# Second attention of a vision tower: scores one step deep in 64-row tiles, projections and output products as jobs between the steps

## The chip, the cores and the metric

One core of one Trainium2 chip runs the whole model. The metric is the device time of one execution in microseconds (us); lower is better. TensorE (PE in the profile, PEld for its weight loads) multiplies matrices into the eight banks of PSUM, VectorE (DVE) and ScalarE (ACT) work on PSUM and SBUF, GpSimd (POOL) on SBUF alone, SyncE (SP) issues transfers. Each engine runs its own instructions in order and waits for the others at semaphores.

## The reference

An image batch of 8 gives 8 x 64 tokens of width 192. A vision-transformer block, a mixture of four attention experts, a mixture of eight feed-forward experts, a second attention and class-wise experts follow, with layer norms between. The change touches the four attention experts:

```
def _L0_attn_ref(x, wq, wk, wv, wo, w_gate, w_up):
    ...
    for e in range(wq.shape[0]):
        q = (x @ wq[e].T).reshape(b, s, nh, hd).transpose(0, 2, 1, 3)
        k = (x @ wk[e].T).reshape(b, s, nh, hd).transpose(0, 2, 1, 3)
        v = (x @ wv[e].T).reshape(b, s, nh, hd).transpose(0, 2, 1, 3)
        scores = jnp.einsum('bhqd,bhkd->bhqk', q, k) * scale
        scores = jnp.where(mask, scores, NEG)
        attn = jax.nn.softmax(scores, axis=-1)
        o = jnp.einsum('bhqk,bhkd->bhqd', attn, v)
        o = o.transpose(0, 2, 1, 3).reshape(b, s, h)
        outs.append(o @ wo[e].T)
    fused = jnp.concatenate(outs, axis=-1)
    gate = jax.nn.silu(fused @ w_gate.T)
    value = fused @ w_up.T
    return gate * value
```

Here b = 8 images, s = 64 tokens each, nh = 12 heads of hd = 16, four experts; with 64 tokens a window of 64 makes the mask plain causal. All of it is fp32.

## The kernel before

The program is one list of instructions per engine, written by hand; the order in each list is that of the loops in the code, and a semaphore (`s[name]`) counts what another engine has finished. All matrix products go through the helper at L1363 and all transposes through the one at L1367, so rows of the trace name these lines; the fillers that keep TensorE's clock up are at L1375.

The second attention runs over 4 experts (e) of 4 steps (t) each, n = 4e + t in all; a step handles two images. Heads are worked in six pairs. The names:

- `project1(e)`: Q and K of all tokens, three blocks of 128 output rows into banks 3, 4, 5. `q_out` (VectorE, L1011) copies Q twice, each copy with the other head of every pair set to zero by the mask `parity`; `k_out` (ACT, L688) copies K in pieces of 32 rows into the block-diagonal operands `kbd` and `kbdB`, which POOL has filled with zeros.
- `values_in(e)`: V into banks 5 and 6; `v_out` (ACT, L700) copies it into `vbd`.
- `scores1(n)`: for each of two images one product of 256 and one of 128 columns, into banks 3 and 4 for even n, 5 and 6 for odd n.
- `softmax1_in(n)` (VectorE): scale and causal mask out of PSUM (L1023), maximum (L1028), subtraction (L1029); `exp1` (ACT, L707).
- `turn1(n)`: six transposes of the weights into banks 0 and 1, `pT1_out` (ACT, L713) copies them; `values1(n)`: six products of 66 columns (values and the sum for two heads) into bank 7; `out1(n)` (VectorE, L1039, L1042) divides by the sum.
- `turn_o(n)`: two transposes of the output into bank 2, `oT_out` (VectorE, L1052) copies every second step; `join(e, c)`: the output product of the expert, in two parts of 128 and 64 rows, through bank 2; copied by ACT (L748) and VectorE (L1087).
- `gate_up(i, ...)`: the gate and value products of token tile i over the four experts, at the end.

In TensorE's order, scores run up to one step ahead of the softmax they feed and the value product one step behind. The projection of the next expert stands as one block in step t = 3, ahead of the value product of the step before, and its V block follows the first scores in t = 0:

```
                if t == 0:
                    scores1(n)
                    values_in(e)
...
                    else:
...
                    elif e < EA - 1:
                        project1(e + 1)
                    values1(n - 1)
```

Before all this, at the start of the program, POOL makes constants one after the other (`link` waits for each), VectorE waits for the last (`consts_made`), makes `parity` from `par_i` (L839 to L842), and then copies the first pixels (L835), which TensorE transposes.

## Time and profile before

| | us |
|---|---|
| median of 3 runs | 443.72 (442.05 to 443.74) |
| the profiled execution, its own time | 443.94 |
| its span, first to last instruction | 442.2 |
| TensorE busy | 414.3 |
| VectorE busy | 246.7 |
| ACT busy | 166.4 |
| mean granted TensorE clock, share of full | 0.979 |

The span is shorter than the execution's time by what lies around the first and last instruction. Busy time of an engine says how long instructions of it were on record, not that it ran at its peak: ends of matrix products are modelled. Second attention begins at 107.3 us in the span and ends some 130 us later.

### The profile page before, as it was taken

The numbers are of one execution on the slowest core, as the hardware profiler recorded it, in microseconds if no ns is written. First come the engines' busy times: TensorE is split into PE (matmuls) and PEld (weight loads), VectorE is DVE, ScalarE is ACT, GpSimd is POOL, SyncE is SP. The second block draws the span as 40 slices with busy tenths as digits, with TensorE's granted clock in tenths as the row PEclk, the third lists the DMA queues.
The fourth block names the chain that finished last, engine by engine and source line by source line (L and its number), as shares of the span: only waits on it lengthen the run. The fifth ranks groups of instructions, "written<-read, shape, count | busy, mean of one in ns | idle before, by whom it ended". The sixth has DMA issues, their size and how long they took to land.

```text
span 442.2 us, 7376 instructions
## 1 busy us (share of the span) xinstructions
PE 414.3 (94%) x2913; PEld 340.6 (77%) x2913; DVE 246.7 (56%) x718; ACT 166.4 (38%) x264; POOL 51.7 (12%) x107
## 2 busy tenths in 40 slices
PE   8989998998789999999999899999999999998993
PEld 8958886785577859578646579988998899697683
DVE  2457565413487857768445464585558215467423
ACT  1236433624436444354311382353334311711420
POOL 7132011270000000000001130000000201204002
PEclk9999999999899999999999899999999999969899
DMA  8999200000297000000000993244221000000001
GB/s 203 257 219 235 53 3 1 1 0 19 77 288 183 0 2 0 1 0 1 1 1 12 270 278 89 87 125 126 64 63 54 2 0 1 0 4 0 1 1 36
DMA packets 28656, 30.51 MB, mean 69 GB/s; under 512 B 4867, under 2 KB 24073, under 8 KB 28622
## 3 DMA queue, kind: packets, MB, share of 16 engines
q1 hardware_dynamic: 28072, 29.82, 26.6%
q8 instruction: 23, 0.38, 0.4%
q10 hardware_dynamic: 390, 0.22, 0.2%
q14 instruction: 11, 0.09, 0.1%
q0 software_dynamic: 160, 0.01, 0.0%
HBM read 29.63 MB, written 0.39 MB: 68 GB/s over the span
## 4 chain that ended last, share of the span: by engine, by line
PE 78%; DVE 12%; issue 4%; ACT 3%; POOL 2%; DVEq 0%; POOLq 0%; ACTq 0%
PE ps L1363 71%; PE ps L1367 6%; DVE front L1023 2%; DVE front L1028 2%; DVE bn L882 1%; PE ps L1375 1%; ACT front L688 1%; ACT front L624 1%; POOL rstd L486 1%; DVE xn L897 1%; DVE mv L885 1%; DVE front L1042 1%; DVE front L1052 0%; DVE front L1087 0%; DVE wide L1235 0%
## 5 line engine op out<-in xcount | busy, mean ns | idle before, releaser
L1363 PE MATMUL ps<-front 64*64 64x64 f32 (+4 forms) x848 | 80.7, 269 | 6.2 <-ACT front L688 2.1
L1363 PEld LDWEIGHTS ps<-front 128*128 128x128 f32 (+1 forms) x848 | 73.2, 165 | 14.7 <-issue 4.5
L1363 PE MATMUL ps<-halves 128*128 128x512 f32 x330 | 80.9, 400 | 2.3 <-ACT halves L593 1.8
L1363 PEld LDWEIGHTS ps<-halves 128*128 128x128 f32 x330 | 61.5, 190 | 15.9 <-issue 2.0
L1363 PE MATMUL ps<-wide,front 128*128 128x192 f32 x432 | 72.0, 327 | 0.0
L1363 PEld LDWEIGHTS ps<-wide,front 128*128 128x128 f32 x432 | 70.3, 190 | 1.0 <-issue 0.5
L669 ACT ACTIVATE front<-ps,colc 128x512 f32<-128x512 f32 x60 | 40.1, 689 | 52.7 <-PE ps L1363 52.5
L1367 PE MATMUL ps<-ident,front 128*128 128x128 f32 (+1 forms) x192 | 27.6, 272 | 2.9 <-DVE front L1087 1.9
L485 POOL TENSOR_SCALAR rstd<-mv 128x2 f32<-128x2 f32 (+1 forms) x15 | 3.3, 218 | 227.1 <-DVE mv L885 227.1
L1367 PEld LDWEIGHTS ps<-ident,front 128*128 128x128 f32 (+1 forms) x192 | 21.5, 140 | 8.2 <-issue 4.2
L1183 DVE SCALAR_TENSOR_TENSOR xn<-ps,small,xn 128x192 f32<-128x192 f32 x28 | 9.8, 410 | 31.0 <-PE ps L1363 31.0
L713 ACT ACTIVATE front<-ps 128x768 f32<-128x768 f32 x16 | 13.0, 810 | 26.1 <-PE ps L1367 25.8
L1375 PE MATMUL ps<-ident 128*128 128x128 f32 x156 | 21.1, 299 | 1.6 <-POOL ident L439 1.6
L1363 PE MATMUL ps<-xT,turned 128*128 128x512 f32 x48 | 21.3, 594 | 1.0 <-DVE xT L1003 1.0
L1375 PEld LDWEIGHTS ps<-ident 128*128 128x128 f32 x156 | 20.6, 215 | 1.9 <-POOL ident L439 1.6
L1023 DVE SCALAR_TENSOR_TENSOR front<-ps,causal 128x384 f32<-128x384 f32 x32 | 16.3, 550 | 10.2 <-PE ps L1363 10.2
L1011 DVE TENSOR_SCALAR front<-ps,parity 128x512 f32<-128x512 f32 (+1 forms) x16 | 11.2, 742 | 15.3 <-PE ps L1363 15.3
L1363 PE MATMUL ps<-front,xT 128*128 128x128 f32 (+2 forms) x176 | 17.5, 270 | 2.2 <-ACT xT L595 1.3
L1363 PEld LDWEIGHTS ps<-front,xT 128*128 128x128 f32 (+1 forms) x176 | 16.8, 171 | 3.1 <-ACT xT L595 1.6
L1363 PE MATMUL ps<-turned,front 128*128 128x384 f32 (+2 forms) x52 | 18.5, 499 | 0.0
L688 ACT ACTIVATE front<-ps 32x512 f32<-32x512 f32 x24 | 14.1, 589 | 9.5 <-PE ps L1363 9.2
L1363 PEld LDWEIGHTS ps<-xT,turned 128*128 128x128 f32 x48 | 8.8, 190 | 10.8 <-issue 10.8
(255 smaller groups left out, 546.8 us busy)
## 6 DMA issues: line engine op xcount, KB each, us to landing
wide<-in_w SPq DMA_DIRECT2D x8, 576.0 KB, 4.7
wide<-in_w SPq DMA_DIRECT2D x8, 384.0 KB, 5.6
wide<-in_w SPq DMA_DIRECT2D x16, 192.0 KB, 6.1
front<-in_a2w SPq DMA_DIRECT2D x5, 576.0 KB
front<-in_a1w SPq DMA_DIRECT2D x5, 384.0 KB
front<-in_x SPq DMA_DIRECT2D x3, 512.0 KB, 7.5
front<-in_w_qkv SPq DMA_DIRECT2D x2, 576.0 KB, 7.1
front<-in_a1w SPq DMA_DIRECT2D x5, 192.0 KB
```

Of the source, the lines that this page charges most:

```text
L486: tell(pool.tensor_tensor(rstd[0:rows, i], rstd[0:rows, i], neghalf[0:rows, i], ALU.pow), "rstd_ready")
L624: act.activation(pT0[:, hp % 2].rearrange("p a b -> p (a b)"), ps[:, 5, :], ACT.Copy).then_inc(s["pT0_done"], 1)
L669: act.activation(dst[:, f, :], ps[:, bank, :], func, bias=col(bias0 + f)).then_inc(s["h_act"], 1)
L688: ins = act.activation((kbdB if c else kbd)[r, :, g, :], src.rearrange("p (b j) -> p b j", b=B), ACT.Copy)
L713: act.activation(pT1[:, n % 2].rearrange("p (a b) c -> p a (b c)", a=2), ps[:, 0:2, 0:3 * P], ACT.Copy).then_inc(s["pT1_done"], 1)
L1011: ins = dve.tensor_scalar(qm[0:n, c, :, h, :], ps[0:n, 3 + 2 * c, :].rearrange("p (b i) -> p b i", b=B), parity[0:n, h:h + 1], None, ALU.mult)
L1023: ins = dve.scalar_tensor_tensor(p1[:, k, :, m, :], ps[:, 3 + 2 * k + m, 0:PAIRS * S].rearrange("p (a j) -> p a j", a=PAIRS), DH ** -0.5, ...
L1028: link(dve.tensor_reduce(mx1[:, k, :], pk, AX.X, ALU.max))
L1183: return dve.scalar_tensor_tensor(dst[:, i, :], two_t(4 + 2 * (e % 2), i), comb[:, i, e:e + 1], xn[:, i, :], ALU.mult, ALU.add)
L1363: return pe.matmul(o, l, r, start=start, stop=stop)
L1367: return pe.transpose(o, i, ident[0:k, 0:k])
L1375: pe.matmul(ps[:, bank, 0:P], ident[:, :], ident[:, :], start=True, stop=True)
```

## The change

It concerns the second attention alone, and the constants at the start.

- `scores1(n)` writes banks 3 and 4 for every n, so it waits until VectorE has read step n - 1. It is six products of 128 columns over 64 rows each: rows 0 to 63 of the operands give bank 3, rows 64 to 127 bank 4. `scores1(n + 1)` is the first thing of step n.
- Q and K are now stored twice (one set per parity of e), as `qm` and `kb` without zero fills: ACT's `qk_out` copies each block twice with a mask (`parity` for Q, `pair` for K). VectorE copies no Q any more. The third block of `project1` is eight products of 256 columns that write 64 rows each.
- The projection of expert e + 1 is cut into jobs between `turn1(n)` and `values1(n)`: blocks 0 and 1 at t = 0, block 2 at t = 2, V at t = 3; both parts of `join(e - 1)` at t = 1. They use banks 5 and 6. `values1(n)` now belongs to step n. In the last expert two `gate_up` tiles take the places of the jobs at t = 2 and 3.
- The mask is added in three instructions and the scale goes into exp.
- POOL drops three fills and makes one more iota; VectorE makes the mask `pair` from it.

The diff, cut; of functions that are written anew, the removed lines (they stand in the listing above) are left out.

```diff
-        kbd = take(B, 4, S)
-        kbdB = take(B, 2, S)
+        kb = take(2, B, 2, S), take(2, B // 2, 2, S)
...
-        qm = take(2, B, 2, S)
+        qm = take(2, B, 2, S), take(2, B // 2, 2, S)
...
             link(pool.iota(par_i[:, :], pattern=[[0, 1]], base=0, channel_multiplier=1))
+            link(pool.iota(pair_i[:, :], pattern=[[0, 1]], base=0, channel_multiplier=1))
...
-            link(pool.memset(kbd, 0.0))
-            link(pool.memset(kbdB, 0.0))
-            link(pool.memset(qm[DB:P, 1], 0.0))
...
+            def split_by(mask, x, n):
+
+                for y in range(2):
+                    ins = act.activation(x[:, :, y, :], n.rearrange("p (b i) -> p b i", i=S), ACT.Copy,
+                                         scale=mask[:, y:y + 1])
+                return ins
+
+            def qk_out(e, x):
+
+                act.wait_ge(s["qk1_mm"], 3 * e + x + 1)
+                k = e % 2
+                if x == 0:
+                    ins = split_by(parity, qm[0][:, k], ps[:, 6, :])
+                elif x == 1:
+                    ins = split_by(pair, kb[0][:, k], ps[:, 5, :])
+                else:
+                    split_by(parity, qm[1][:, k], ps[:, 6, 0:4 * S])
+                    ins = split_by(pair, kb[1][:, k], ps[:, 6, 4 * S:8 * S])
+                ins.then_inc(s["qk1_done"], 1)
...
+            def fT_out(e):
+
+                act.wait_ge(s["wo1_mm"], 2 * e + 1)
+                act.activation(fT[:, e, 0, :], ps[:, 6 if e < EA - 1 else 2, :], ACT.Copy).then_inc(s["fT_act"], 1)
 
             def exp1(n):
                 act.wait_ge(s["sub1"], n + 1)
-                act.activation(p1[:, n % 2], p1[:, n % 2], ACT.Exp).then_inc(s["exp1"], 1)
+                act.activation(p1[:, n % 2], p1[:, n % 2], ACT.Exp, scale=DH ** -0.5).then_inc(s["exp1"], 1)
...
+            for x in range(3):
+                qk_out(0, x)
+            v_out(0, 0)
             exp1(0)
+            v_out(0, 1)
             N1 = NT * EA
+            for n in range(N1):
                 e, t = divmod(n, NT)
+                pT1_out(n)
+                if e < EA - 1:
+                    if t == 0:
+                        qk_out(e + 1, 0)
+                    elif t == 2:
+                        qk_out(e + 1, 2)
+                    elif t == 3:
+                        v_out(e + 1, 0)
+                if t == 1 and e >= 1:
+                    fT_out(e - 1)
+                if n + 1 < N1:
                     exp1(n + 1)
+                if e < EA - 1:
+                    if t == 0:
+                        qk_out(e + 1, 1)
+                    elif t == 3:
+                        v_out(e + 1, 1)
+                elif t in (2, 3):
 
                     act.wait_ge(s["v1_mm"], 2 * EA)
+                    w1_high(t - 2)
+            fT_out(EA - 1)
...
+            link(dve.tensor_scalar(pair_i[:, :], pair_i[:, :], 5, 1, ALU.logical_shift_right, ALU.bitwise_and))
+            link(dve.tensor_copy(pair[:, 1:2], pair_i[:, :]))
+            link(dve.tensor_scalar(pair[:, 0:1], pair[:, 1:2], -1.0, 1.0, ALU.mult, ALU.add))
...
-                for m in range(2):
-                    ins = dve.scalar_tensor_tensor(
-                        p1[:, k, :, m, :], ps[:, 3 + 2 * k + m, 0:PAIRS * S].rearrange("p (a j) -> p a j", a=PAIRS),
-                        DH ** -0.5, causal[:, :].unsqueeze(1).to_broadcast([P, PAIRS, S]), ALU.mult, ALU.add)
+                mask = causal[:, :].unsqueeze(1).unsqueeze(1).to_broadcast([P, 2, 2, S])
+                for half in range(2):
+                    dve.tensor_tensor(p1[:, k, 2 * half:2 * half + 2].rearrange("p a m j -> p m a j"),
+                                      ps[:, 3 + half, 0:4 * S].rearrange("p (m a j) -> p m a j", m=2, a=2), mask, ALU.add)
+                ins = dve.tensor_tensor(p1[:, k, 4:6].rearrange("p a m j -> p m a j"),
+                                        ps[:, 3:5, 4 * S:6 * S].rearrange("p m (a j) -> p m a j", a=2), mask, ALU.add)
...
+            for n in range(N1):
                 e, t = divmod(n, NT)
+                if n + 1 < N1:
                     softmax1_in(n + 1)
+                if n % 2 == 0 and n >= 2:
+                    oT_out(n // 2 - 1)
+                if t == 1 and e >= 1:
+                    fT_low(e - 1)
+                out1(n)
+            oT_out(2 * EA - 1)
+            w1_low(0)
+            w1_low(1)
+            fT_low(EA - 1)
...
+            def project1(e, x):
+
+                if x == 0 and e >= 1:
+                    pe.wait_ge(s["v1_done"], 2 * e)
+                if x == 2:
+                    pe.wait_ge(s["qk1_done"], 3 * e + 1)
+                    if e >= 2:
+                        pe.wait_ge(s["fT_act"], e - 1)
+                if x < 2:
+                    for k in range(2):
+                        ins = mm(ps[:, 6 - x, :], wT[e][:, k, x * P:(x + 1) * P], xT[:, k, :], k == 0, k == 1)
+                else:
                     for m in range(2):
+                        at = 2 * P + DB * m
+                        for k in range(2):
+                            for half in range(2):
+                                ins = mm(ps[DB * half:DB * half + DB, 6, 4 * S * m:4 * S * (m + 1)],
+                                         wT[e][:, k, at:at + DB],
+                                         xT[:, k, :].rearrange("p (b n) -> p b n", n=S)[:, half:B:2, :], k == 0, k == 1)
+                ins.then_inc(s["qk1_mm"], 1)
+
+            def values_in(e, j):
+
+                pe.wait_ge(s["qk1_done"], 3 * e + 2 + j)
+                if j == 0 and e >= 2:
+                    pe.wait_ge(s["fT_dve"], e - 1)
+                for m in range(2):
+                    i = 2 * j + m
+                    for k in range(2):
+                        ins = mm(ps[:, 5 + j, m * D:m * D + D], xT[:, k, i * P:(i + 1) * P],
+                                 wT[e][:, k, 2 * D:3 * D], k == 0, k == 1)
+                ins.then_inc(s["v1_mm"], 1)
 
             def scores1(n):
                 e, t = divmod(n, NT)
                 if t == 0:
+                    pe.wait_ge(s["qk1_done"], 3 * e + 3)
+                if n >= 1:
+                    pe.wait_ge(s["s1_read"], n)
+                for c, m in ((0, 0), (0, 1), (1, 0)):
+                    for half in range(2):
+                        r = slice(DB * half, DB * half + DB)
+                        b, at = t if c else 2 * t + m, (2 * c + m) * P
+                        ins = mm(ps[:, 3 + half, at:at + P], qm[c][r, e % 2, b].rearrange("p h i -> p (h i)"),
+                                 kb[c][r, e % 2, b].rearrange("p a j -> p (a j)"), True, True)
                 ins.then_inc(s["s1_mm"], 1)
...
-                if n % NT == 0 and n >= NT:
-                    pe.wait_ge(s["fT_dve"], n // NT)
...
+                last = e == EA - 1
                 if c == 0:
                     pe.wait_ge(s["ot1_done"], 2 * e + 2)
-                else:
-                    pe.wait_ge(s["fT_act"], e + 1)
+                if not last:
+                    if e + 2 < EA:
+                        pe.wait_ge(s["qk1_done"], 3 * (e + 2) + 1 + c)
+                    else:
+                        pe.wait_ge(s["v1_done"], 2 * EA)
                 r0, n = CH[c]
                 at = DB * (e % 2) if c else 0
+                bank = (2, 0)[c] if last else 6 - c
                 for h in range(2):
-                    ins = mm(ps[at:at + n, 2, :], woT[e][0:96, h, r0:r0 + n], oT1[0:96, h, :], h == 0, h == 1)
+                    ins = mm(ps[at:at + n, bank, :], woT[e][0:96, h, r0:r0 + n], oT1[0:96, h, :], h == 0, h == 1)
...
+            first = ((0, 0), (1, 0), (2, 0), (0, 1))
+            for x in range(3):
+                project1(0, x)
+            values_in(0, 0)
+            scores1(0)
+            values_in(0, 1)
             N1 = EA * NT
             for n in range(N1):
                 e, t = divmod(n, NT)
+                if n + 1 < N1:
                     scores1(n + 1)
                 turn1(n)
+                if e < EA - 1:
+                    if t == 0:
+                        project1(e + 1, 0)
+                        project1(e + 1, 1)
+                    elif t == 2:
+                        project1(e + 1, 2)
+                    elif t == 3:
+                        values_in(e + 1, 0)
+                        values_in(e + 1, 1)
+                if n >= 1:
                     turn_o(n - 1)
+                if t == 1 and e >= 1:
+                    join(e - 1, 0)
+                    join(e - 1, 1)
+                if e == EA - 1 and t >= 2:
+                    pe.wait_ge(s["fT_act"], EA - 1)
+                    pe.wait_ge(s["fT_dve"], EA - 1)
+                    gate_up(t, first)
+                values1(n)
+
             pe.wait_ge(s["s1_read"], N1)
             gate_up(0, first)
+            turn_o(N1 - 1)
             gate_up(1, first)
             join(EA - 1, 0)
             join(EA - 1, 1)
```

How the change moves instructions, at three places. The rows are those of each engine's list: line, instruction, output and inputs, partitions x columns of the output, how many in a row, and the semaphores waited for.

TensorE, start of expert 0, from behind the projection (before) or its first two blocks (after) to the transposes of step 0 (`ps` is PSUM, `xT` the tokens, `turned` the weights, `front` the attention's operands). Before:

```order
L1363 MATMUL ps<-front 128x256 [waits qk1_act,qk1_dve]
L1363 MATMUL ps<-front 128x128
L1363 MATMUL ps<-front 128x256
L1363 MATMUL ps<-front 128x128
L1363 MATMUL ps<-turned,xT 128x192 x8
L1363 MATMUL ps<-front 128x256 [waits v1_done]
L1363 MATMUL ps<-front 128x128
L1363 MATMUL ps<-front 128x256
L1363 MATMUL ps<-front 128x128
L1367 MATMUL ps<-ident,front 128x128 [waits exp1]
```

After:

```order
L1371 MATMUL ps<-xT,turned 64x256 [waits qk1_done]
L1371 MATMUL ps<-xT,turned 64x256 x7
L1371 MATMUL ps<-turned,xT 128x192 [waits qk1_done]
L1371 MATMUL ps<-turned,xT 128x192 x3
L1371 MATMUL ps<-front 128x128 [waits qk1_done]
L1371 MATMUL ps<-front 128x128 x5
L1371 MATMUL ps<-turned,xT 128x192 [waits qk1_done]
L1371 MATMUL ps<-turned,xT 128x192 x3
L1371 MATMUL ps<-front 128x128 [waits s1_read]
L1371 MATMUL ps<-front 128x128 x5
L1375 MATMUL ps<-ident,front 128x128 [waits exp1]
```

The third block of the projection waits for the copy of the first; V comes in two parts around the first scores; `scores1(1)` waits for VectorE's read of step 0, and the transposes of step 0 follow it.

TensorE, expert 1, from the transposes of one step to those of the next. Before (t = 2 and 3; the projection of expert 2 is the block of 4 and 2):

```order
L1367 MATMUL ps<-ident,front 128x128 [waits pT1_done,exp1]
L1367 MATMUL ps<-ident,front 128x128 x5
L1367 MATMUL ps<-ident,front 96x128 [waits fT_dve,ot1_done,o1_done]
L1367 MATMUL ps<-ident,front 96x128
L1363 MATMUL ps<-xT,turned 128x512 x4
L1363 MATMUL ps<-xT,turned 128x512 [waits s1_read]
L1363 MATMUL ps<-xT,turned 128x512
L1363 MATMUL ps<-front 128x66 [waits o1_done,v1_done,pT1_done]
L1363 MATMUL ps<-front 128x66 x5
L1367 MATMUL ps<-ident,front 128x128 [waits pT1_done,exp1]
L1367 MATMUL ps<-ident,front 128x128 x5
```

After (t = 0 and 1; the projection's first two blocks are the job):

```order
L1375 MATMUL ps<-ident,front 128x128 [waits pT1_done,exp1]
L1375 MATMUL ps<-ident,front 128x128 x5
L1371 MATMUL ps<-xT,turned 128x512 [waits v1_done]
L1371 MATMUL ps<-xT,turned 128x512 x3
L1375 MATMUL ps<-ident,front 96x128 [waits o1_done]
L1375 MATMUL ps<-ident,front 96x128
L1371 MATMUL ps<-front 128x66 [waits o1_done,v1_done,pT1_done]
L1371 MATMUL ps<-front 128x66 x5
L1371 MATMUL ps<-front 128x128 [waits s1_read]
L1371 MATMUL ps<-front 128x128 x5
L1375 MATMUL ps<-ident,front 128x128 [waits pT1_done,exp1]
L1375 MATMUL ps<-ident,front 128x128 x5
```

The job stands between the transposes and the value product of the same step, and the scores, six products on 64 rows, stand between full-array work on both sides.

ACT, from the exp of expert 0's last step to the middle of expert 1 (L707 and L716 are exp, L713 and L722 the copy of the transposes, L688 and L680 the copies of K, and of Q and K, L700 and L704 of V, L748 and L712 of the output product). Before:

```order
L707 ACTIVATE front<-front 128x768 [waits sub1]
L688 ACTIVATE front<-ps 32x8x64 [waits s1_mm,qk1_mm]
L688 ACTIVATE front<-ps 32x8x64 x3
L688 ACTIVATE front<-ps 32x8x64 [waits qk1_mm]
L688 ACTIVATE front<-ps 32x8x64
L713 ACTIVATE front<-ps 128x768 [waits pv1_mm,t1_mm]
L700 ACTIVATE front<-ps 64x12x32 [waits v1_mm]
L700 ACTIVATE front<-ps 64x12x32
L700 ACTIVATE front<-ps 64x12x32 [waits v1_mm]
L700 ACTIVATE front<-ps 64x12x32
L707 ACTIVATE front<-front 128x768 [waits sub1]
```

After:

```order
L716 ACTIVATE front<-front 128x768 [waits sub1]
L704 ACTIVATE front<-ps 64x12x32 [waits v1_mm]
L704 ACTIVATE front<-ps 64x12x32
L722 ACTIVATE front<-ps 128x768 [waits pv1_mm,t1_mm]
L680 ACTIVATE front<-ps,parity 128x8x64 [waits qk1_mm]
L680 ACTIVATE front<-ps,parity 128x8x64
L716 ACTIVATE front<-front 128x768 [waits sub1]
L680 ACTIVATE front<-ps,pair 128x8x64 [waits qk1_mm]
L680 ACTIVATE front<-ps,pair 128x8x64
L722 ACTIVATE front<-ps 128x768 [waits pv1_mm,t1_mm]
L712 ACTIVATE front<-ps 128x512 [waits wo1_mm]
```

Copies of the next expert's operands stand between the copy of the transposes and the next exp, in place of a block around the change of expert.

## Rows read from the trace of the kernel before

**Rows 1.** The page, busy us and share of the span by engine.

```profile
PE 414.3 (94%) x2913; PEld 340.6 (77%) x2913; DVE 246.7 (56%) x718; ACT 166.4 (38%) x264; POOL 51.7 (12%) x107
```

**Rows 2.** Busy time by stretch: length, then each engine, TensorE clock, DMA share, GB/s.

```profile
107.30:122.00 14.70, 11.45 (x37) 7.89 (x38) 5.74 (x8) 8.23 (x18) 1.07 (x2) 0.88 0.31 82
...
160.00:200.00 40.00, 39.23 (x223) 30.07 (x222) 27.83 (x50) 19.77 (x32) 0.00 (x0) 1.00 0.00 1
```

**Rows 3.** Chain of waits, experts 1 and 2: start us, us, what ran.

```profile
159.72 6.44 PE ps L1363 x24
...
173.90 1.03 DVE front L1023 x2
...
174.95 0.96 DVE front L1028
...
186.59 6.44 PE ps L1363 x24
```

**Rows 4.** Timeline, TensorE, expert 1: start us, us, instructions, [idle before, releaser].

```profile
141.30 2.77 PE L1363 MATMUL ps<-turned,xT 128*128 128x192 f32 x16
...
143.90 1.45 PE L1363 MATMUL ps<-front 128*128 128x66 f32 x12
...
145.19 0.38 PE L1367 MATMUL ps<-ident,front 128*96 128x128 f32 x2
...
145.41 1.47 PE L1363 MATMUL ps<-front 128*128 128x256 f32 x8
...
146.72 1.04 PE L1367 MATMUL ps<-ident,front 128*128 128x128 f32 x8
```

**Rows 5.** Timeline, TensorE, expert 0.

```profile
114.85 1.62 PE L1363 MATMUL ps<-front 128*128 128x256 f32 x8 [2.13 <-ACT front L688]
...
116.26 4.42 PE L1363 MATMUL ps<-turned,xT 128*128 128x192 f32 x16
...
121.76 1.57 PE L1363 MATMUL ps<-front 128*128 128x256 f32 x8 [1.08 <-ACT front L700]
...
127.31 0.88 PE L1367 MATMUL ps<-ident,front 128*128 128x128 f32 x6 [0.71 <-ACT front L707]
...
130.34 1.52 PE L1363 MATMUL ps<-front 128*128 128x66 f32 x12 [0.85 <-DVE front L1042]
```

**Rows 6.** Timeline of weight loads, 64*64 tiles; busy time by stretch, 32*128 tiles.

```profile
55.08 0.56 PEld L1363 LDWEIGHTS ps<-front 64*64 64x64 f32 x32 [0.17 <-issue]
...
387.19:388.98 1.79, 1.79 (x52) 1.79 (x54) 1.28 (x2) 0.37 (x1) 0.00 (x0) 1.00 0.04 9
```

**Rows 7.** Timeline, token transposes that alternate between array shapes.

```profile
374.48 0.44 PE L1367 MATMUL ps<-ident,xn 128*128 128x128 f32 x2
...
374.85 0.43 PE L1363 MATMUL ps<-ident,xn 128*64 128x128 f32 x2
```

**Rows 8.** The page, costliest groups, and one exp from the timeline.

```profile
L713 ACT ACTIVATE front<-ps 128x768 f32<-128x768 f32 x16 | 13.0, 810 | 26.1 <-PE ps L1367 25.8
...
L1023 DVE SCALAR_TENSOR_TENSOR front<-ps,causal 128x384 f32<-128x384 f32 x32 | 16.3, 550 | 10.2 <-PE ps L1363 10.2
L1011 DVE TENSOR_SCALAR front<-ps,parity 128x512 f32<-128x512 f32 (+1 forms) x16 | 11.2, 742 | 15.3 <-PE ps L1363 15.3
...
L688 ACT ACTIVATE front<-ps 32x512 f32<-32x512 f32 x24 | 14.1, 589 | 9.5 <-PE ps L1363 9.2
...
133.27 0.83 ACT L707 ACTIVATE front<-front 128x768 f32<-128x768 f32 x1
```

**Rows 9.** Chain of waits at the start; last zero fills on POOL from the timeline.

```profile
2.02 0.15 POOL par_i L443
...
6.41 0.16 DVE par_i L839
...
6.97 0.25 DVE dist L842
...
7.82 1.09 PE ps L1367 x8
...
97.88 0.72 POOL L525 MEMSET front<- 64x24 f32 x4
```

More of the change, by code:

```diff
@@ L93, in vit_tower @@
         parity = sb("parity", [P, 2])
+        pair_i = sb("pair_i", [P, 1], I32)
+        pair = sb("pair", [P, 2])
         bc = {n: sb("bc_" + n, [P, D]) for n in
@@ L675, in _ @@
             act.activation(xT[:, 0, :], ps[:, 6, :], ACT.Copy).then_inc(s["xT_act"], 1)
-            def k_out(e):
-                for c, (r0, n) in enumerate(CH):
-                    act.wait_ge(s["qk1_mm"], 3 * e + c + 2)
-                    if c == 0 and e >= 1:
-                        act.wait_ge(s["s1_mm"], NT * e)
-                    for g in range(n // 32):
-                        r = slice(32 * g, 32 * g + 32)
-                        src = ps[DB + 32 * g:DB + 32 * g + 32, 5, :] if c else ps[r, 4, :]
-                        ins = act.activation((kbdB if c else kbd)[r, :, g, :],
-                                             src.rearrange("p (b j) -> p b j", b=B), ACT.Copy)
-                    ins.then_inc(s["qk1_act"], 1)
@@ L692, in v_out @@
-            def v_out(e):
-                for j in range(2):
-                    act.wait_ge(s["v1_mm"], 2 * e + j + 1)
-                    if j == 0 and e >= 2:
-                        act.wait_ge(s["pv1_mm"], NT * (e - 1))
-                    for im in range(2):
-                        r = slice(64 * im, 64 * im + 64)
-                        ins = act.activation(
-                            vbd[r, e % 2, 2 * j:2 * j + 2, :, im, 0:2 * DH],
-                            ps[r, 5 + j, 0:2 * D].rearrange("p (m a d) -> p m a d", m=2, a=PAIRS), ACT.Copy)
-                    ins.then_inc(s["v1_done"], 1)
+            def split_by(mask, x, n):
[3 more added lines that the diff above has]
+                return ins
@@ new lines, in v_out @@
+            def v_out(e, j):
+                act.wait_ge(s["v1_mm"], 2 * e + j + 1)
+                if j == 0 and e >= 2:
+                    act.wait_ge(s["pv1_mm"], NT * (e - 1))
+                for im in range(2):
+                    r = slice(64 * im, 64 * im + 64)
+                    ins = act.activation(
+                        vbd[r, e % 2, 2 * j:2 * j + 2, :, im, 0:2 * DH],
+                        ps[r, 5 + j, 0:2 * D].rearrange("p (m a d) -> p m a d", m=2, a=PAIRS), ACT.Copy)
+                ins.then_inc(s["v1_done"], 1)
```

106 lines of the change are left out of this document (6 added, 100 removed).

## Prediction

> **What bounds the kernel now.** The busy table comes first: TensorE works 94% of the span, VectorE 56% [rows 1]. Second, the busy time by stretch: inside the second attention, which begins at 107.3 us, TensorE reads 39.23 of 40 us busy [rows 2]. Ends of products are modelled there, so short waits hide in it, and I take lengths from one start to the next. Third, the chain of waits: one expert repeats after 186.59 - 159.72 = 26.87 us, and between TensorE's pieces it runs through VectorE's mask-and-scale (L1023) [rows 3]. So TensorE is the bound, with gaps in which it waits for the softmax chain.
>
> What is work and what is gap? An fp32 product shows as two records, a transpose as one. From starts [rows 4]: the value projection of an expert (16 records) takes 143.90 - 141.30 = 2.60 us; the scores of a step (8 records) 1.31; a transpose 0.11, so six 0.65; the value product of a step (12 records) 1.29, though it streams only 66 columns: 0.11 per record is the time of its 128-column weight load; the Q and K projection (12 records of 512 columns) 5.15, since the chain's piece of 24 records, 6.44, holds it and one value product [rows 3]; the transposes of the output 0.22; an output product (4 such records of 512, 5.15 / 12 = 0.43 each) 1.72. Per expert: 5.15 + 2.60 + 4 x (1.31 + 0.65 + 1.29 + 0.22) + 2 x 1.72 = 25.1, and with 0.35 for the turn to 64-column tiles and back (priced below) 25.4. That leaves 1.5 us of gaps for each of experts 1 to 3, 4.4 together. The start of expert 0 has its own: 2.1 (K copies), 1.1 (V copies), 0.7 (exp), 0.9 (VectorE), 4.8 in all [rows 5]. Sum 9.2 us. And there the value projection takes 4.42 instead of 2.60 because the granted clock falls to half after the 2.1 us wait: mean 0.88 over 14.7 us, 1.8 us lost [rows 2, 5].
>
> **The change, part by part.**
>
> Scores. Four products (256 + 128 columns, twice) become six of 128 columns, each on 64 rows of the array, alternately upper and lower half. If the halves ran in turn, 12 records x 0.11 = 1.3 us, as now. The trace has no 64x128 tiles, but it has neighbours on both sides. 64x64 tiles: 32 weight loads in 0.56 us, 0.0175 each, where one 128-column load takes 0.11. 32x128 tiles: about 50 records in 1.79 us, 0.036 each; with two of the four tiles holding four of every twelve records, that is 4 x 0.11 / 12, exactly what tiles working side by side give when each pays its own load [rows 6]. So I take 6 records per tile x 0.112 = 0.67 us, 0.64 less per step: 16 x 0.64 = **-10.2**. Bounds: 0 (no overlap) and -10.2.
>
> Turns of the array. Now every scores block stands between full-array work: 32 turns more. The trace turns at 373.8 to 375.6: two records of 128 columns, 0.22 us back to back, take 374.85 - 374.48 = 0.37 with a turn each [rows 7], so a turn costs 0.147, a 64-column load laid open (half of 0.11) included. With a 128-column load open it is 0.055 more: 0.20. 32 x 0.20 = **+6.4**. The Trainium skill, TensorEngine Tiling (Array Packing), Key Properties, says that changing the tiling mode drains TensorE; the trace agrees that a turn costs, and the page prices nothing. The last third of Q and K is projected in 64-column halves as well: 8 products of 256 columns, two side by side, 1.7 us as now; its two turns, 0.15 + 0.20, four times: **+1.4**. The output product has its two before and after.
>
> Gaps. What is now a block (5.15 us of projection, with VectorE's and ACT's copies behind it) becomes jobs between transposes and value product. In a step without a job, the next transposes need, from the end of the scores: 0.2 for the results to land, VectorE 1.14 and two passes of 0.96, ACT's exp 0.83 [rows 3, 8], 4.2 with handovers. TensorE has 0.65 + 0.22 + 1.29, three turns of 0.2 and scores of 0.67: 3.4. And the value product waits for ACT's copy of the transposes, 0.2 + 0.81 - 0.22 = 0.8, in the same step. The two overlap: about 1 us of gap. Any job (3.4 of projection at t = 0, 1.7 at t = 2, 2.6 of values at t = 3, 3.4 of output product at t = 1) covers it. Jobless are only t = 1 of expert 0 and t = 0 of expert 3: 2 x 1.0. At the start: Q's copy 0.2, V's and the rest 0.5, exp(0) behind 3 us of softmax 1.8 (scores(1) alone is cover). At the end the last output transposes wait 0.6, one step 0.2. Sum 5.3 instead of 9.2; VectorE and ACT are no bound: VectorE is busy 27.83 of 40 us now, 18.7 per expert [rows 2], and loses the four Q copies of 0.74; ACT 19.77 of 40, 13.3 per expert, gets eight Q and K copies for six K copies of 0.59, at most 1.2 more [rows 8]. Both stay far below TensorE. **-3.9**. Bounds: 0 and -5.5. What is late next is TensorE itself: 25.4 - 4 x 0.64 + 4 x 0.4 + 0.35 = 24.8 us per expert, 2.1 below now.
>
> VectorE's mask is now three adds of 256 columns instead of two of 384 at 0.55 [rows 8]. Each costs between 0.37 (by columns) and 0.55 (by instruction); I take 0.38, 1.14 instead of 1.02 to 1.10 a step. Its cover is TensorE's work; without the cover it would be 16 x 0.1.
>
> Clock. Half a clock cost 1.8 us after a wait of 2.1; a wait of 1.1 left it full. The longest is now 1.8. Undecided, so half of it: **-0.9**, bounds 0 and -1.8.
>
> Start of the program. POOL gets one more iota, 0.15 + 0.05, ahead of the semaphore that VectorE waits for; VectorE three more tiny instructions, 6.97 - 6.41 = 0.56, ahead of the first pixel copy, which TensorE's first transposes wait for [rows 9]. That is on the chain and TensorE runs on from there: **+0.75**. Bounds 0 and +0.75. POOL's three zero fills, which go, lay before its last ones at 97.88, and their readers begin at 107.3: nothing.
>
> The end: the gate products of two token tiles move up between the last steps, where they are jobs; their total is the same. DMA issues keep their order.
>
> **Sum**: -10.2 + 6.4 + 1.4 - 3.9 - 0.9 + 0.75 = -6.5 us. On the profiled execution's own 443.94 that is 437.4; the median of the runs shown, 443.72, lies 0.2 lower. I forecast 437.2.
>
> **The rivals.**
>
> A, slower: the half tiles take turns. All neighbours in the trace have 64 rows and 64 columns or 32 rows; two streams of 128 columns into two banks are in none. Then 10.2 does not come and the turns stay: 447.4. The sum breaks even when the block takes 0.67 + 6.5 / 16 = 1.08 us, so two thirds of the overlap would have to be lost. Against it: both neighbours run at full overlap [rows 6]. Chance 0.10.
>
> B, the gaps stay: the Q and K copies stand on ACT between the copy of the transposes and the exp of the next step, and two scores banks instead of four tie scores(n+1) to VectorE's read of n. If that makes as many gaps as it removes, 3.9 is lost: 441.1. For it: VectorE's chain is already on the path. Against it: every job is longer than the 1 us to be covered. Chance 0.15.
>
> C, a turn waits for the last product to leave the array. A pair of transposes lasts 0.38, so one record 0.27 from start to end, against 0.11 between starts [rows 4]; then a turn is 0.16 + 0.11 = 0.27 and 40 turns cost 2.8 more: 440.0. That is the strict reading of the Trainium skill's drain (same page and section). Against it: the turns of [rows 7] would then take 0.16 + 0.055 = 0.22 each, and they take 0.147. Chance 0.08.
>
> **How the numbers follow.** Forecast 0.67, A 0.10, B 0.15, C 0.08. The range goes from 433.0 (turns at 0.15 take 2.2 off, full clock 0.9, fewer gaps 1.1) to 443.0 (B with the clock lost and part of C), leaving out A and a little more above (0.12) and some 0.08 below. About 0.5% of this kernel, 2.2 us, is what a measurement can tell from no change: faster means below 441.5. The forecast, C and half of B with some tail lie there: 0.77; between 441.5 and 445.9 0.14; slower 0.09, nearly all of it A.
>
> **What would show it.** After the change: first records of a scores block to the following transpose some 1.0 to 1.1 us, its 12 records in 0.7; one expert every 24.5 to 25; a gap of 0.1 to 0.2 on the load row at each turn; no wait over 0.3 us in experts 1 and 2; waits near 1.8 once at the start; the first pixel copy 0.75 later. The forecast is wrong if the 12 records take 1.3 (A), if waits for exp or for the transposes' copy stand in most steps (B), or if turns cost 0.27 (C).

## The result and the profile after

The changed kernel takes 436.26 us (434.90 to 439.94, 4 runs) beside 443.70 before: a ratio of 0.985, 95% interval 0.981 to 0.990, so 7.4 us less. I had forecast 437.2, with 433.0 to 443.0 as the range. The profiled execution took 436.5 (span 434.8); the sum, made on the profiled 443.94, gave 437.4.

The page's busy line, to be read beside [rows 1]:

```profile
PE 408.7 (94%) x3025; PEld 332.6 (77%) x3025; DVE 238.3 (55%) x721; ACT 168.4 (39%) x272; POOL 48.2 (11%) x105
```

TensorE's share has not moved. It executes 112 instructions more and is busy 5.6 us less.

Where did the 7.4 go? The second attention's projection begins at 108.20 (before 107.34). The filler products behind the stage begin at 229.35 (before 236.68):

```profile
229.35 3.29 PE L1383 MATMUL ps<-ident 128*128 128x128 f32 x28
```

So the stage shrank from 129.34 to 121.15, by 8.2 us; the start of the program costs 0.9; what follows the filler's start is as long as before (205.45 and 205.52).

One expert, in the chain of waits [rows 3]:

```profile
157.95 0.81 PE ps L1375 x6
...
162.27 0.02 issue
162.29 0.94 PE ps L1371 x12
163.23 0.80 PE ps L1375 x6
...
182.59 0.80 PE ps L1375 x6
```

An expert takes 182.59 - 157.95 = 24.64 us, against 26.87. From 133.23 to 192.80, which holds experts 1 and 2, the chain is TensorE's alone, but for 0.02 or 0.03 of issue at three places; VectorE has left it there. The scores are the piece at 162.29: the next piece starts 0.94 behind it in the chain, and by the timeline what follows a block of scores starts 0.87 behind its first record (117.12 and 117.99).

In step 12, which has no job, the chain leaves TensorE and runs through VectorE's softmax and exp back to the next transposes:

```profile
192.83 0.24 DVE front L1050
...
193.85 0.76 DVE front L1033 x2
...
196.95 0.85 ACT front L716
...
197.85 1.09 PE ps L1375 x8
```

TensorE's timeline has the waits that are left [rows 4, 5]:

```profile
108.20 7.25 PE L1371 MATMUL ps<-xT,turned 128*128 128x512 f32 x24 [1.04 <-DVE xT L1023]
...
117.12 0.94 PE L1371 MATMUL ps<-front 64*128 64x128 f32 x12 [0.17 <-ACT front L680]
...
122.17 0.87 PE L1375 MATMUL ps<-ident,front 128*128 128x128 f32 x6 [1.75 <-ACT front L716]
...
130.75 2.42 PE L1371 MATMUL ps<-front 128*128 128x66 f32 x24 [0.68 <-ACT front L722]
...
187.80 0.88 PE L1375 MATMUL ps<-ident,front 128*128 128x128 f32 x6
...
193.59 1.09 PE L1375 MATMUL ps<-ident,front 128*128 128x128 f32 x8
195.36 2.42 PE L1371 MATMUL ps<-front 128*128 128x66 f32 x24 [0.68 <-ACT front L722]
197.85 1.09 PE L1375 MATMUL ps<-ident,front 128*128 128x128 f32 x8
...
210.85 0.42 PE L1375 MATMUL ps<-ident,front 128*96 128x128 f32 x2 [0.43 <-DVE front L1053]
```

Exp (L716) is waited for at the start; the copy of the transposes (L722) twice, in the steps without a job (1 and 12); VectorE's output (L1053) once near the end. A step is counted here from its first transpose to that of the next one: step 12 lasts 197.85 - 193.59 = 4.26.

Busy time by stretch [rows 2]. The third number from the end is the granted clock:

```profile
108.20:112.00 3.80, 3.80 (x5) 1.62 (x6) 0.00 (x0) 2.63 (x8) 1.07 (x2) 0.55 0.25 58
112.00:229.35 117.35, 113.31 (x748) 80.71 (x747) 76.80 (x152) 56.84 (x92) 0.00 (x0) 1.00 0.20 52
```

The stage still has one low stretch. It now lies at its very beginning, behind the waits of 0.65 and 1.04 for the tokens, and the 1.75 us wait has none behind it. In the profile before, it lay between 116 and 120.

Groups by line with shapes kept apart [rows 8]:

```profile
L1033 DVE TENSOR_TENSOR front<-ps,causal 128x256 f32<-128x256 f32 x32 | 12.1, 419 | 10.7 <-PE ps L1371 10.2
...
L1035 DVE TENSOR_TENSOR front<-ps,causal 128x256 f32<-128x256 f32 x16 | 6.6, 415 | 0.0
...
L680 ACT ACTIVATE front<-ps,parity 128x512 f32<-128x512 f32 x8 | 5.1, 683 | 4.2 <-PE ps L1371 4.2
```

And the chain at the program's start [rows 9]:

```profile
2.23 0.15 POOL pair_i L445
...
6.62 0.17 DVE par_i L856
...
7.75 0.20 DVE dist L862
7.94 0.77 DVE front L852
8.76 1.09 PE ps L1375 x8
```

### The profile page after: what moved, and what is told of

It reads as the page before. It is cut to its first block, busy times and chain, and to the rows that moved or that the text cites. A ratio compares the mean times of both kernels' runs of the same rounds, so it can differ in the third digit from the quotient of the medians.

```text
span 434.8 us, 7607 instructions
## 1 busy us (share of the span) xinstructions
PE 408.7 (94%) x3025; PEld 332.6 (77%) x3025; DVE 238.3 (55%) x721; ACT 168.4 (39%) x272; POOL 48.2 (11%) x105
## 4 chain that ended last, share of the span: by engine, by line
PE 82%; DVE 9%; ACT 4%; issue 2%; POOL 2%; DVEq 0%; POOLq 0%; ACTq 0%
PE ps L1371 73%; PE ps L1375 7%; DVE bn L902 1%; PE ps L1383 1%; DVE front L1040 1%; DVE front L1039 1%; ACT front L623 1%; POOL rstd L488 1%; DVE xn L917 1%; ACT front L716 1%; DVE mv L905 1%; DVE front L1033 1%; DVE wide L1243 0%; DVE tok L991 0%; ACT front L680 0%
## 5 line engine op out<-in xcount | busy, mean ns | idle before, releaser
L1371 PE MATMUL ps<-front 64*64 64x64 f32 (+3 forms) x912 | 71.8, 265 | 3.8 <-ACT front L722 1.4
L1371 PEld LDWEIGHTS ps<-front 64*64 64x64 f32 (+2 forms) x912 | 64.8, 166 | 12.6 <-issue 4.9
L1375 PE MATMUL ps<-ident,front 128*128 128x128 f32 (+1 forms) x192 | 28.6, 276 | 4.0 <-ACT front L716 1.7
L1371 PE MATMUL ps<-xT,turned 128*64 128x256 f32 (+1 forms) x96 | 24.0, 476 | 1.2 <-DVE xT L1023 1.0
L722 ACT ACTIVATE front<-ps 128x768 f32<-128x768 f32 x16 | 13.0, 810 | 25.6 <-PE ps L1375 25.6
L1371 PEld LDWEIGHTS ps<-xT,turned 128*64 128x64 f32 (+1 forms) x96 | 10.6, 161 | 11.5 <-issue 8.6
L1033 DVE TENSOR_TENSOR front<-ps,causal 128x256 f32<-128x256 f32 x32 | 12.1, 419 | 10.7 <-PE ps L1371 10.2
L716 ACT ACTIVATE front<-front 128x768 f32<-128x768 f32 x16 | 13.5, 845 | 8.6 <-DVE front L1040 8.5
L1040 DVE TENSOR_TENSOR front<-front 128x768 f32<-128x768 f32 x16 | 15.3, 958 | 0.6
```

Source lines behind the costliest of these rows:

```text
L716: act.activation(p1[:, n % 2], p1[:, n % 2], ACT.Exp, scale=DH ** -0.5).then_inc(s["exp1"], 1)
L722: act.activation(pT1[:, n % 2].rearrange("p (a b) c -> p a (b c)", a=2), ps[:, 0:2, 0:3 * P], ACT.Copy).then_inc(s["pT1_done"], 1)
L1033: dve.tensor_tensor(p1[:, k, 2 * half:2 * half + 2].rearrange("p a m j -> p m a j"), ps[:, 3 + half, 0:4 * S].rearrange("p (m a j) -> p m ...
L1040: dve.tensor_tensor(pk, pk, mx1[:, k, :].unsqueeze(2).to_broadcast([P, 2 * PAIRS, S]), ALU.subtract).then_inc(s["sub1"], 1)
L1371: return pe.matmul(o, l, r, start=start, stop=stop)
L1375: return pe.transpose(o, i, ident[0:k, 0:k])
```

## The experiments

Each starts from the changed kernel unless it says otherwise. Ratios are to the kernel before, with 95% intervals; the change itself has 0.985 (0.981 to 0.990). Most kernels' times fall on levels some 1 to 3 us apart, which go with the mean granted clock (the change: 434.9 at 0.982, 436.5 at 0.978, 439.9 at 0.970). So where a microsecond is the question, I read lengths in the trace; where two profiles differ by a low stretch of the clock within the stage, the text says so.

**halves_in_turn.** Do the halves overlap whatever the order?

```diff
-                for c, m in ((0, 0), (0, 1), (1, 0)):
-                    for half in range(2):
+                for half in range(2):
+                    for c, m in ((0, 0), (0, 1), (1, 0)):
```

> Leaves the same six products, tiles and banks, and issues the three of the upper half first, then the three of the lower half. Theory (products lie side by side only where neighbours in the order go to different halves): 12 records at 0.112 us in place of 6 pairs at 0.105, so the block's records take 1.3 instead of 0.65 and 16 x 0.67 = 10.7 us come back: 447. Rival (the array overlaps the halves in whatever order they come): 436.3, no change. Second rival (the gain came from fewer waits and not from the scores): less than 3 us.

439.41 us, ratio 0.992 (0.989 to 0.994). Neither theory. What follows a block starts 1.19 behind its first record instead of 0.87, 16 x 0.32 = 5.1 us. In the trace the second half does not wait for the first to end; it starts 0.33 behind it, after three of its six records, and the last three run alone. Some overlap survives the bad order, half is lost. The stage, 108.56 to 234.30, is 4.6 us longer than the change's: the wait for exp at its start, 1.41 instead of 1.75, swallows 0.34 of it. The medians differ by 3.2 only.

**same_half.** The whole overlap taken away, all else left:

```diff
-                        r = slice(DB * half, DB * half + DB)
+                        r = slice(0, DB)
```

> All six score products read rows 0 to 63, so every one of them uses the upper half of the array; three of six scores are then computed from the wrong heads. Work, banks, turns and waits stay. Theory of the sum (the overlap of the halves is worth 0.67 a step, the records then follow each other at 0.11): 16 x 0.67 = 10.7 more than the change, 447. halves_in_turn gave 0.33 a step, since the second half started after three records of the first. Rival (products into two banks overlap whatever rows they use, the banks and not the halves are what counts): 436.3. Second rival (part of it is hidden behind VectorE's chain): 440 to 444.

446.26 us, ratio 1.006 (1.003 to 1.010): 10.0 above the change. The stage, 110.15 to 239.32 and all at full clock, takes 129.17 us where fillers (below) takes 119.49 at full clock: 9.7 more, with 0.67 less of waiting for exp. Two neighbouring transposes of its timeline:

```profile
179.43 2.98 PE L1371 MATMUL ps<-front 128*128 128x66 f32 x24
182.34 1.09 PE L1375 MATMUL ps<-ident,front 128*128 128x128 f32 x8
```

Value product and scores take 2.91, in the change 2.25 in the same step (175.56 minus the start in the next fence). 16 x 0.66 = 10.6: that is what rival A would have cost. The banks are the same as in the change, so it is the halves that count and not the banks. Without the overlap the change would have been slower than the kernel before.

```profile
173.31 2.32 PE L1371 MATMUL ps<-front 128*128 128x66 f32 x24
```

**extra_full and extra_half.** The price of a turn: one product more per step, on 128 rows or on 64.

```diff
                 for p in range(PAIRS):
+                    if p == 3:
+                        mm(ps[:, 0, 3 * P:4 * P], ident[0:P, :], ident[0:P, :], True, True)
```

(extra_half reads `ident[0:DB, :]` twice.)

> One product without use (128 rows, 128 columns, identity times identity) stands between the third and the fourth transpose of every step. Two records of 0.11: 16 x 0.22 = 3.5 us, 439.8, if TensorE sets the pace in every step. It is the measure for extra_half. If VectorE or ACT set the pace in most steps: under 1.5 us more.

> The same product without use on 64 rows of the array, so that each step has two turns more, and two records of 0.105. Against extra_full it differs by 32 turns alone. Theory of the sum (0.20 a turn): 6.4 more than extra_full, 446.2. By the starts in the trace of the change (0.24 a turn for a scores block): 7.7 more, 447.5. A turn that waits for the last product to leave the array (0.27): 8.6 more, 448.4. If turns cost nothing and only their loads do: 0 to 1 more.

439.47 us, 0.992 (0.988 to 0.995), and 444.31, 1.002 (1.000 to 1.004). The first is 3.2 above the change (2.9 in the stage), near the 3.5 foreseen. The two differ by 4.8, less than any theory but the last. From the transposes to the job behind them, extra_full then extra_half:

```profile
164.29 0.55 PE L1375 MATMUL ps<-ident,front 128*128 128x128 f32 x3
164.67 0.39 PE L1371 MATMUL ps<-ident 128*128 128x128 f32 x2
164.90 0.49 PE L1375 MATMUL ps<-ident,front 128*128 128x128 f32 x3
165.22 2.77 PE L1371 MATMUL ps<-turned,xT 128*128 128x192 f32 x16
```

```profile
168.07 0.55 PE L1375 MATMUL ps<-ident,front 128*128 128x128 f32 x3
168.54 0.48 PE L1371 MATMUL ps<-ident 64*128 64x128 f32 x2
168.96 0.55 PE L1375 MATMUL ps<-ident,front 128*128 128x128 f32 x3
169.34 2.77 PE L1371 MATMUL ps<-turned,xT 128*128 128x192 f32 x16
```

0.93 and 1.27: two turns cost 0.34, a turn 0.17. In step 0 the wait for V's copies swallows them and in step 15 the wait for VectorE's output; in the other fourteen, steps 1 and 12 among them, they count: 28 x 0.17 = 4.8 us, as the medians say. (The stages differ by 6.5, because extra_half has one low stretch more, at clock 0.77 from 120 to 124 us and 0.81 from 124 to 128.) Rival C (0.27) falls: it would make 7.6. The Trainium skill, TensorEngine Tiling (Array Packing), Key Properties, has the array drained at a change of mode; the records agree that a turn costs and not that it costs a product's full way through the array.

**x2_full.** The last third of Q and K without its turns:

```diff
-                    for m in range(2):
...
+                    for k in range(2):
+                        ins = mm(ps[:, 6, :], wT[e][:, k, 2 * P:3 * P], xT[:, k, :], k == 0, k == 1)
```

> The last third of Q and K is projected by two full-array products of 512 columns instead of eight 64-column tiles; its values then stand in other places, so the scores use other numbers for two of six head pairs. Theory (its price is its two turns, 0.22 each by the trace's starts): four times 0.44 = 1.8 us less, 434.5; with the one at the stage's start hidden behind the copies' wait, 1.3 less, 434.9. Rival (TensorE's turns there are hidden behind VectorE and ACT): 436.3.

436.23 us, 0.983 (0.977 to 0.989): no gain that can be told, the rival's answer. The trace says what became of it:

```profile
156.88 1.88 PE L1371 MATMUL ps<-xT,turned 128*128 128x512 f32 x4
158.60 0.38 PE L1375 MATMUL ps<-ident,front 128*96 128x128 f32 x2
158.82 1.45 PE L1371 MATMUL ps<-front 128*128 128x66 f32 x12
160.43 0.94 PE L1371 MATMUL ps<-front 64*128 64x128 f32 x12 [0.16 <-ACT front L680]
...
181.36 1.88 PE L1371 MATMUL ps<-xT,turned 128*128 128x512 f32 x4
```

An expert takes 181.36 - 156.88 = 24.48, 0.16 less. From the transposes of this step over the job to the value product, TensorE needs 0.29 less than in the change. After the job it has only the output transposes and a value product before the next expert's first scores, which need ACT's copies of it: from value product to transposes 2.47 (158.82 to 161.29) instead of 2.34. So 0.13 of the 0.29 comes back as a wait.

**jobs_moved and jobs_everywhere.** Jobs for the jobless steps. The core of jobs_moved on TensorE:

```diff
                         project1(e + 1, 0)
+                    if n == 1 or (t == 0 and e >= 1):
                         project1(e + 1, 1)
...
-                        values_in(e + 1, 1)
+                        if e < EA - 2:
+                            values_in(e + 1, 1)
+                elif t == 0:
+                    values_in(e, 1)
```

jobs_everywhere adds, with expert 1's other jobs one per step:

```diff
+                if n == 0:
+                    project1(1, 1)
                 turn1(n)
```

> The two steps without a job get one: K of expert 1 moves from step 0 to step 1, the second half of V of expert 3 from step 11 to step 12. Theory (a jobless step waits 0.68 for ACT's copy of the transposes and a job covers it): 2 x 0.68 = 1.4 us less, 434.9. Rival (the step that loses its job, or half of it, waits instead): 436.3.

> As jobs_moved, and expert 1's K projection moves ahead of the first transposes, where TensorE waits 1.75 for exp; the other jobs of expert 0 move so that each step has one. Theory: 1.75 + 0.68 + 0.68 = 3.1 less, less some 0.2 for ACT's copies standing before exp(1): 433.2 to 433.5. Rival (VectorE's softmax chain at the start is the bound, and TensorE only waits later instead): the wait comes back at exp(1), 434.9 as jobs_moved, or 436.3.

435.80 us, 0.981 (0.978 to 0.985), and 431.91, 0.974 (0.970 to 0.978). The median of jobs_moved, 0.5 below the change, can't tell theory from rival; the traces can. The filler behind the stage, of jobs_moved and of jobs_everywhere:

```profile
227.30 3.29 PE L1385 MATMUL ps<-ident 128*128 128x128 f32 x28
```

```profile
223.73 3.29 PE L1392 MATMUL ps<-ident 128*128 128x128 f32 x28
```

In jobs_moved the stage begins at 108.29 and has the same low stretch as the change: 119.01 us instead of 121.15, so 2.14 less, 1.07 for each step that got a job. (Its profile has another low stretch at 347 us, which the change's has not.) In jobs_everywhere the stage begins at 108.20 and takes 115.53, all of it at full clock. fillers (below) has the change's order at full clock and takes 119.49: 3.96 less. Theory's 3.1 was made from the waits shown (0.68 each), and they are not all. A step without a job lasts 4.26; step 11, with the value projection's 2.60 taken off (187.80 to 193.59, 5.79), 3.19: the difference is 1.07 again. It has two parts. The value product starts 1.77 behind the transposes instead of 0.93, 0.84 later; the line shows 0.68 of it, as the modelled end of the record ahead covers the rest. And the next transposes start 2.49 behind the value product instead of 2.25, 0.24 later, because they wait for exp, at the end of the chain shown for step 12. 1.75 + 2 x 1.07 = 3.9.

**one_block.** The projection in one piece again, in step 2:

```diff
-                    if t == 0:
+                    if t == 2:
                         project1(e + 1, 0)
                         project1(e + 1, 1)
-                    elif t == 2:
                         project1(e + 1, 2)
...
```

(ACT's copies move with it, and the waits for the two banks.)

> All of the next expert's Q and K projection stands in step 2 as one job of 5.2 us; steps 0 have no job any more, and the waits for the two banks follow the values' copies instead. Theory (a step without a job waits 0.7 for ACT's copy of the transposes, and nothing else): steps 0, 4 and 8 join 1 and 12, 3 x 0.7 = 2.1 more, and up to 0.5 each for the copies of Q and K before the next expert's first scores: 438.4 to 439.9. Rival (TensorE is busy enough in any order): 436.3. Second rival (the block is what the kernel before had, and all 3.9 us of the gap term come back): 440.2.

444.33 us, ratio 0.999 (0.996 to 1.003), runs from 439.02 to 448.50. The fastest, at clock 0.977, agrees with the theory (the change had 436.03 at 0.977); the median is 5 us above, and at a lower clock. Its profile (443.1 of span) gives the stretch:

```profile
108.23:119.00 10.77, 10.39 (x64) 6.51 (x64) 2.38 (x5) 7.31 (x17) 1.08 (x2) 1.00 0.25 58
119.00:135.00 16.00, 13.08 (x68) 11.55 (x69) 9.50 (x21) 5.13 (x7) 0.00 (x0) 0.56 0.90 240
135.00:150.00 15.00, 14.98 (x96) 10.70 (x96) 6.91 (x13) 9.14 (x16) 0.00 (x0) 0.90 0.47 120
```

Without jobs in steps 0 and 1, waits of 1.75, 0.90 and 0.47 follow each other, and behind the first of them TensorE is at 1.2 GHz for some 17 us (14 in the second stretch, 3 in the third). The jobs' worth is the waits they cover and, it seems, the clock: nine of the twelve runs are at 0.968 or below, which no run of the change is. That it is the row of waits which keeps the clock down is argued from this one profile.

**fillers.** Does the clock fall because of the waits ahead of the stage?

```diff
...
+            keep_busy(3, 0)
             pe.wait_ge(s["tok_done"], 4)
             turn_tokens(tok, 3)
+            keep_busy(5, 0)
             xT_ready(3)
...
```

(The two waits for the weights' copies, which stood behind, now stand ahead of these lines.)

> Three and five products without use stand in TensorE's two waits (0.65 and 1.04 us) ahead of the second attention. In the profile of the change the clock is half from 108.5 to 111.9, right behind these waits. Theory A (the waits let it fall): the stage begins at full clock in every run and 1.7 us go, 434.6. Theory B (how many low stretches a run has is not decided by these two waits, since the kernel before had them too and kept its clock there): one falls elsewhere, 436.3 and the same spread. If a filler runs past the end of a wait: 0.1 to 0.2 more.

437.29 us, 0.987 (0.984 to 0.991): theory B. The page's clock row of 40 slices, fillers first, the change below:

```profile
PEclk9999999999999999999998999999999989969899
```

```profile
PEclk9999999999899999999999899999999999969899
```

In its profile (436.22) the slice at 109 us has no low stretch any more (the stage runs at full clock from end to end), and the one at 348 us, 9 in the change, has one. The spread is as wide as before (434.8 to 439.8). With the waits filled, this profile has as many low stretches as the change's; that the filling itself sent one from 109 us to 348 is not shown, as each kernel has one profile. The stage alone, 119.49 us at full clock and 121.15 with one low stretch, prices such a stretch at 1.7 us.

**pair_later and consts_later.** The start:

```diff
             dve.wait_ge(s["consts_made"], 1)
...
-            link(dve.tensor_scalar(pair_i[:, :], pair_i[:, :], 5, 1, ALU.logical_shift_right, ALU.bitwise_and))
-            link(dve.tensor_copy(pair[:, 1:2], pair_i[:, :]))
-            link(dve.tensor_scalar(pair[:, 0:1], pair[:, 1:2], -1.0, 1.0, ALU.mult, ALU.add))
```

(they stand behind the pixel copies instead; consts_later takes the wait and the other four there too)

> The iota of the second mask is made after the zero fills that follow the constants, and VectorE's three small instructions on it after the pixel copies. Theory (the start of the program is on the chain and TensorE runs on from there): the first pixel copy 0.7 to 0.8 us earlier, and the end as well, 0.9 in all with the longer copy: 435.4 to 435.6. Rival (the stage waits for something later, such as the tokens or the weights' copies): 436.3.

> As pair_later, and the first mask, the distances and the wait for the constants move behind the pixel copies too, so that the first copy waits for the pixels alone. If the chain starts with VectorE's wait for GpSimd's constants (6.62): the copy starts when the pixels have landed, which the trace does not show; if they are there by 6.0, 1.9 us less than the change, 434.4. If they land at 7.0 or later, no more than pair_later gives.

435.68 us, 0.982 (0.979 to 0.985), and 433.64, 0.978 (0.975 to 0.981). TensorE's first transposes of pixels start at 7.83 in pair_later, at 8.76 in the change, at 7.82 before. (pair_later's stage begins at 108.97 all the same, since its profile has a low stretch ahead of it, 0.88 over 20 to 34 us.) VectorE's pixel copy and TensorE in consts_later:

```profile
5.45 0.71 DVE L852 COPY front<-front 128x1024 f32<-128x1024 f32 x1 [5.45 <-DMA front<-in_x]
...
7.07 1.04 PE L1374 MATMUL ps<-ident,front 128*128 128x128 f32 x8
...
106.50 3.24 PE L1370 MATMUL ps<-xT,turned 128*128 128x512 f32 x7 [1.04 <-DVE xT L1022]
```

(The window cuts the last row short.) 1.7 us earlier at the start and 1.7 at the stage, 99 us later: the start is on the chain, one for one. The pixels are there at 5.45 and copied at 6.16, but the transposes start only at 7.07. In between TensorE works at the fillers that stand ahead of them, and the chain of waits now comes from there:

```profile
1.58 5.65 PE ps L1382 x28
```

**all_three.** consts_later, jobs_everywhere and fillers together.

> consts_later, jobs_everywhere and fillers in one kernel. If they add up on the medians measured so far (433.64 and 431.91 against 436.26): 2.6 + 4.4 less, 429.3, and 1.7 less again if theory A of fillers holds, 427.6. By the traces, which show 1.7 and 3.1 to be had (the rest of jobs_everywhere's gain being clock): 431.4.

429.64 us (427.87 to 430.87, 6 runs), ratio 0.969 (0.966 to 0.972). The stage, 106.70 to 222.23, takes 115.53 again. It beats both kernels, 6.6 below the change and 14 below the kernel before, and agrees with the sum of the medians (429.3). What fillers gives in it was not measured apart; alone it gave nothing.

## Why the prediction was right, point by point

- **Scores and their turns** (-10.2 + 6.4 = -3.8 predicted). The overlap was sized right: 0.66 by same_half where I took 0.64. A turn costs 0.17 with one product between two turns, where I took 0.20. From last value record to first transpose, with the record's own time taken off and the slower second transpose put on, scores and turns together are 1.02 in most steps (1.11 behind some), for 1.31 before: some -4.5. Right, a little undersized. One reading of the prediction is false: the trace before does have tiles of 64 rows by 128 columns, in transposes. They follow each other at about 0.07 us and no two lie side by side, so they would not have priced the overlap:

```profile
100.96 0.56 PE L1367 MATMUL ps<-ident,wide 64*128 64x64 f32 x6
...
101.36 0.27 PE L1367 MATMUL ps<-ident,front 64*96 64x64 f32 x2
```

- **The last third's turns** (+1.4). Measured by x2_full, stage against stage at full clock: 119.49 - 119.02 = 0.5. This term was mis-sized: I put 0.35 for both turns on the path of every expert; they measure 0.29, and 0.13 of it lies in a wait for ACT's copies that I had not seen. The fourth pair, at the stage's start, gave nothing that shows.
- **Gaps** (-3.9, to 5.3 left). TensorE's timeline shows no wait in experts 1 and 2, as said. Two jobless steps at 1.07 each, where I took 1.0, and from the two parts that I had named, the softmax chain of 4.2 and the copy of the transposes; exp at the start 1.75, where I took 1.8; 0.17 for Q's copies; 0.43 for the last output transposes, where I took 0.6. Together 4.5 of the 9.2 are left, -4.7. The other way round, the stage's -8.2 less the two terms above leaves -4.2; the waits shown need not be all. Rival B falls, by these waits and by the stage of jobs_moved.
- **Mask adds.** Three of 0.42 busy each, which overlap: from the first to the maximum behind them 1.12 (118.17 to 119.29), where I took 1.14 and the kernel before had 1.05. VectorE has left the chain in experts 1 and 2, so it cost nothing there, as argued; where the chain does run through it (step 12, above), it costs under 0.1 each time.
- **Clock** (-0.9, half of 1.8). It gave nothing: this step of the prediction failed. I had tied the loss to the wait of 2.1 us. The longest wait fell to 1.75, and one low stretch was still there, behind other waits (3.80 us at 0.55). Nor does the wait alone decide it: the same 1.75 has no low stretch behind it in the change, in jobs_moved and in fillers, and one in extra_half and in one_block. What does decide it stays open.
- **Program start** (+0.75). The transposes are 0.94 late, 0.86 of it at the stage. The three small instructions and the iota are 0.57 + 0.21 of that; the rest I had not foreseen: the pixel copy itself takes 0.85 in the timeline where it took 0.69 before. Why it is longer stays open; in pair_later it takes 0.68 and the transposes start at 7.83 again.

```profile
7.86 0.85 DVE L852 COPY front<-front 128x1024 f32<-128x1024 f32 x1
```

The sum by what was measured: -4.5 + 0.5 - 4.2 + 0 + 0.9 = -7.3, against -6.5 forecast and -7.4 found. It closes by construction, since -4.2 is what the stage leaves over; with the waits counted one by one it would be -7.8. The mechanism was the one forecast. That the number came within 1 us is in part luck: the scores with their turns, and the last third's turns, were 0.7 and 0.9 too dear in the sum, and a clock term of 0.9 did not come.

## What to carry to other kernels

Products on different halves of the array lie fully side by side when they alternate in the order of issue; in two blocks, half of the overlap was lost here. Count the overlap against two turns of 0.17 us for each block: at 0.11 us saved for each pair of records it pays only above three pairs, by this case's numbers. A step whose only cover is its own work waited at each hand-over, for the copy and for exp: give every step one job, the first ones too. And a mask that is needed at 108 us does not belong ahead of the first copy at 7 us.

## What the runs showed of the hardware that I had not expected

- Three products (six records) in a row on one half of the array do not shut out the other half: it starts after three records (0.33 us), so the wrong order loses half of the overlap (5.1 of 10.6 us) and not all.
- The time of one kernel comes in levels that go with the granted clock (all_three: 427.87 at 0.985, 429.38 at 0.982, 430.87 at 0.979); where a low stretch falls is not settled by one wait.
- A wait of 0.68 in the timeline was 0.84 of time by the starts, since the modelled end of the record ahead reaches into it, and the step lost 1.07: the rest was a wait for exp that the timeline does not mark.
